# Eleven passes with barriers made into one continuous program, with an order of its own for each engine

## The reference, cut to what matters

```
x: [16, 256, 128]
for attn, ffn in ((geo, moe0), (diff, feed-forward + mx), (lora, moe2), (wide, moe3)):
    x = x + attn(norm(x))
    x = x + ffn(norm(x))
geo:  8 heads of 16, causal, a head-wise bias folded into q and k
diff: differential attention across the 32 half heads inside one token, then RMS norm; feed-forward 512; mx-quantised linear
lora: 16 heads of 8, not causal
wide: 16 heads with keys of 128, causal
moe0 / moe2 / moe3: top-1 routing to 8 / 14 / 8 experts, hidden 512 / 256 / 128 (Relu, Gelu, Relu)
moe3: an expert keeps only its first 512 tokens over all sequences, in order
```

## Time and profile before

| | us |
|---|---|
| device time, 3 runs: median | 2933.23 |
| lowest, highest | 2922.30, 2940.96 |
| span of the profiled execution, first to last instruction | 2937.0 |
| TensorE busy | 1974.8 (67%) |
| VectorE busy | 1762.4 (60%) |
| ScalarE busy | 1132.8 (39%) |
| GpSimd busy | 705.2 (24%) |

### The profile page before, as it was taken

How to read it: one execution, slowest core, us unless ns; L and a number is a source line. 1 busy time by engine, 2 the same in 40 slices (tenths; PEclk the granted TensorE clock), 3 DMA queues, 4 the chain that set the end, 5 groups by cost and what they waited for, 6 DMA issues and landing times. The chain is left out here.

```text
span 2937.0 us, 40367 instructions
## 1 busy us (share of the span) xinstructions
PE 1974.8 (67%) x12945; PEld 1381.7 (47%) x12945; DVE 1762.4 (60%) x4295; ACT 1132.8 (39%) x2730; POOL 705.2 (24%) x891
## 2 busy tenths in 40 slices
PE   4555655666978677766776678658775766657593
PEld 4233353345546544564456445645464335435452
DVE  2112856685768576857687667757685777543232
ACT  0112222332555336542554256425542353234261
POOL 1000431143014411442035203530243034100101
PEclk9757566568988788887898788879787876778695
DMA  9112031034103510352026201530153103301502
GB/s 249 24 46 74 1 110 32 1 98 136 23 29 106 150 35 2 107 158 53 2 73 183 62 2 47 173 84 16 39 153 100 22 1 100 89 9 33 142 1 60
DMA packets 183309, 207.84 MB, mean 71 GB/s; under 512 B 19792, under 2 KB 148432, under 8 KB 182640
## 3 DMA queue, kind: packets, MB, share of 16 engines
q1 hardware_dynamic: 165536, 186.19, 23.1%
q0 software_dynamic: 6144, 12.60, 1.4%
q10 hardware_dynamic: 11392, 6.18, 1.0%
HBM read 158.39 MB, written 42.34 MB: 68 GB/s over the span
## 5 line engine op out<-in xcount | busy, mean ns | idle before, releaser
L1450 POOL TENSOR_TENSOR second_room<-second_room 128x512 f32<-128x512 f32 x32 | 47.6, 1486 | 765.1 <-ACT second_room L1332 765.0
L1220 ACT ACTIVATE late_room<-ps,late_neg_max 128x128 f32<-128x128 f32 (+1 forms) x512 | 186.9, 420 | 69.2 <-DVE late_neg_max L1597 63.8
L1622 DVE TENSOR_REDUCE mid_room<-ps 128x2 f32<-128x512 f32 x256 | 165.1, 687 | 55.2 <-PE ps L954 52.0
L1257 ACT ACTIVATE mid_room<-ps 128x512 f32<-128x512 f32 x256 | 142.9, 598 | 132.0 <-PE ps L965 131.8
L1211 ACT ACTIVATE late_room<-ps 128x384 f32<-128x384 f32 x256 | 125.9, 492 | 155.1 <-PE ps L885 151.9
L1596 DVE TENSOR_REDUCE late_neg_max<-ps 128x1 f32<-128x128 f32 x256 | 73.5, 287 | 179.7 <-PE ps L877 179.1
L1779 DVE TENSOR_TENSOR second_room<-second_room 128x1024 f32<-128x1024 f32 x128 | 163.0, 1274 | 13.2 <-ACT second_room L1332 9.7
L1057 PE MATMUL ps<-mid_pool 128*128 128x128 f32 x544 | 107.2, 328 | 87.1 <-DMA mid_pool<-moe_tables 78.0
L875 PE MATMUL ps<-late_aT,heads_T 128*128 128x256 f32 x512 | 164.1, 405 | 0.0
L1783 DVE TENSOR_REDUCE second_room<-second_room 128x256 f32<-128x1024 f32 x128 | 156.2, 1220 | 4.4
L965 PE MATMUL ps<-mid_pool 51*128 51x256 bf16 x512 | 64.7, 338 | 130.9 <-DMA mid_pool<-max_rows 62.2
(11 more groups left out here) (389 smaller groups left out, 5174.4 us busy)
## 6 DMA issues: line engine op xcount, KB each, us to landing
early_pool<-moe_tables SPq DMA_DIRECT2D x88, 578.0 KB
mid_pool<-moe_tables SPq DMA_DIRECT2D x136, 321.0 KB
heads_T<-moe_tables SPq DMA_DIRECT2D x88, 192.5 KB
mid_pool<-mid_room SPq DMA_DIRECT2D x192, 64.0 KB
mid_room<-moe_sorted_in SPq DMA_DIRECT2D x32, 256.0 KB, 3.1
moe_sorted_out<-mid_room SPq DMA_DIRECT2D x32, 256.0 KB
early_room<-moe_sorted_in SPq DMA_DIRECT2D x16, 256.0 KB, 3.1
moe_sorted_out<-early_room SPq DMA_DIRECT2D x16, 256.0 KB, 5.8
```

The costliest lines, as they stand in the source:

```text
L1220: ins = act.activation(probs[s][:, n % RING, qt, 0:w], ps[:, bank, qt * P:qt * P + w], ACT.Exp, bias=neg_max[s][:, n % RING, qt:qt + 1])
L1257: act.activation(probs_T[s][:, n % (2 * QUAD), :], ps[:, B + slots.index(("unit", n)) % s.score_banks(at), :], ACT.Exp)\
L1622: dve.tensor_reduce(all_max[:, :, (h % 2 * 8 + h // 2) * GROUP_SEQS + seq], ps[:, B + n % s.banks, :].rearrange("p (q k) -> p q k", q=2), ...
```

## The change

The passes, the loop, the barriers, the copies of x and the clearing of semaphores are gone. Semaphores now count through the whole program: each is declared with the number of signals it gets per group, and `nth` gives the value to wait for in group g. x lives in a ring of five groups (`xs`, `x_of`), in which all four streams add in place; the next group's x is loaded at the start of EARLY's steps of the group before, and the result is sent from the ring.

Preparation is a fifth stream "P" whose steps stand among EARLY's. x of group 0 and the five loads that EARLY needs come first, then those of moe0, of SECOND, and at last those of MID and LATE. The copies of the tables of moe2 and moe3 stay on ScalarE's queue: its order begins "EEEPP", and they are the second P. On VectorE the order begins "PEPEEPEEPPEPP", on TensorE "EEEEPEEEP", with the 16 products of `wide_m` behind 50 more steps.

`ORDERS` now has one string per engine for the whole program (TensorE 2467 steps, ScalarE 1906, VectorE 1800, GpSimd 217, SP 468). There are no empty steps, and steps are finer (scores, transposes and products with values are steps of their own). Each stream works on group after group without any meeting point. Within the strings the stream with the older group mostly comes first.

Smaller edits: the octets of `back_to_tokens` go one by one instead of in waves; `gate_of_max` of moe0 and moe2 stands behind the signal `slots_ready`; small tiles are shared (`filled`, `starts`, `ends`, `table_of`, `dsq` inside `dhalves`, `max_rows` inside `mid_room`); `result` and the semaphore `result_free` are gone.

```diff
-        def next_turn():
-            nc.gpsimd.dma_reset(range(group_first.num, group_last.num + 1))
-            nc.all_engine_barrier()
-            nc.sync.sem_clear(range(group_first.num, group_last.num + 1))
-            nc.all_engine_barrier()
...
-        with nc.Fori(0, GROUPS - 3) as g:
-            with nc.Block(no_gpsimd_drain=True) as block:
-                group_block(block, list(STREAMS), x_v[:, bass.ds(g * TILES + 3 * TILES, TILES), :],
-                            out_v[:, bass.ds(g * TILES, TILES), :])
-            next_turn()
...
-                for source, target in ((MID, LATE), (SECOND, MID), (EARLY, SECOND)):
-                    if source in streams:
-                        settle()
-                        link(dve.tensor_copy(x[target][:, :, :], x[source][:, :, :]))
...
+def take_steps(engine, programs):
+    running = {letter: itertools.chain.from_iterable(rounds) for letter, rounds in programs.items()}
+    for letter in ORDERS[engine]:
+        next(running[letter])
...
+        def nth(told, g, n):
+            return told, g * a_round[told.name] + n
...
+        xs = sb("xs", [P, X_RING, TILES, DIM])
+        x_of = lambda g: xs[:, g % X_RING, :, :]
...
+        def steps_of(prepare, early, second, mid, late):
+            rounds = {"P": [prepare()]}
+            for s, program in ((EARLY, early), (SECOND, second), (MID, mid), (LATE, late)):
+                rounds[s.letter] = [program(g) for g in range(GROUPS)]
+            return rounds
...
+                def load_x(g):
+                    if g >= 1:
+                        sp.wait_ge(*nth(x_here, g - 1, 16))
+                    if g >= X_RING:
+                        sp.wait_ge(*nth(x_sent, g - X_RING, 16))
+                    sp.dma_start(x_of(g), x_v[:, g * TILES:(g + 1) * TILES, :]).then_inc(x_here, 16)
...
+                def prepare():
+                    act.wait_ge(prepared, LAM_SUMMED)
+                    act.activation(lam_exp[:, :], lam_sum[:, :], ACT.Exp).then_inc(lam_exped, 1)
+                    yield
+                    act.wait_ge(m0_here, 16 * len(m0_loads))
+                    act.wait_ge(second_here, 16 * len(second_loads))
+                    for dst, src in m2_copies + m3_copies:
+                        with nc.allow_non_contiguous_dma(reason="columns of tables, once"):
+                            act.dma_start(dst, src).then_inc(later_built, 16)
+                    yield
...
+                        if n < at.units:
+                            scores(n)
+                            yield
                         if TURN_LAG <= n < at.units + TURN_LAG:
                             turn_probs(n - TURN_LAG)
-                        last = n - VALUES_LAG
-                        if last >= 0 and last % QUAD == QUAD - 1:
-                            values(last // QUAD)
-                        yield
+                            yield
+                        quad, rest_of_quad = divmod(n - VALUES_LAG, QUAD)
+                        if rest_of_quad == QUAD - 1 and quad >= 0:
+                            values(quad)
+                            yield
```

More of the change, by code:

```diff
@@ L21 @@
 GROUPS = SEQS // GROUP_SEQS
+X_RING = 5
 BANK = 512
@@ L109, in score_banks @@
         return self.banks if at is LORA else self.banks - 1
[L111 to L119, removed]
+EARLY = Stream("geo", "E", 0, 2, ["geo_in", "geo_out", "moe0_router"], ["v", "o"])
+SECOND = Stream("diff", "S", 2, 1, ["diff_in", "diff_out", "diff_ff", "mx_in"], ["conn", "ff", "mx"])
+MID = Stream("lora", "M", 3, 2, ["lora_in", "lora_out", "moe2_in"], ["v", "o"])
+LATE = Stream("wide", "L", 5, 3, ["wide_in", "wide_out", "moe3_router"], ["v", "o"])
 STREAMS = (EARLY, SECOND, MID, LATE)
@@ L206, in sequence_model @@
+def take_steps(engine, programs):
+    running = {letter: itertools.chain.from_iterable(rounds) for letter, rounds in programs.items()}
+    for letter in ORDERS[engine]:
+        next(running[letter])
+    for letter, program in running.items():
+        assert next(program, "over") == "over", f"{engine}: {letter} has more steps than the order"
 def sequence_model(nc, a, out):
@@ L700, in take_steps @@
-        def take_steps(streams, programs):
-            letters = "".join(s.name[0].upper() for s in streams)
-            order = ORDERS[letters] if len(streams) > 1 else letters * len(WEIGHTS[streams[0]])
-            for letter in order:
-                next(programs[letters.index(letter)])
-            for program in programs:
-                assert next(program, None) is None, "a program has more steps than weights"
-        def steps(n):
-            for _ in range(n):
-                yield
@@ L1362, in late @@
                                                 lambda b: wide_c[:, b:b + 1])
-                    yield from experts(s, MOE3, "moe3_router")
-                programs = {EARLY: early, SECOND: second, MID: mid, LATE: late}
-                take_steps(streams, [programs[s]() for s in streams])
+                    yield from experts(s, MOE3, g, "moe3_router")
+                take_steps("ACT", steps_of(prepare, early, second, mid, late))
             @block.gpsimd
@@ L1938, in sequence_model @@
[L1938 to L1943 removed]
+                    yield from experts(s, MOE3, g, "moe3_router", m3_br)
+                take_steps("DVE", steps_of(prepare, early, second, mid, late))
```

1443 lines of the change are left out of this document (699 added, 744 removed).

## The result

The changed kernel takes 3241.8 us (median of four runs, 3225.8 to 3245.1) against 2937.1 us before (2922.3 to 2944.1): 1.103 times as long, 95% interval 1.099 to 1.107. The forecast was 2603 us. The profiled execution has a span of 3243.4 us in a run of 3245.1.

The account below looks back on a forecast made before the run. No engine was taken to bound the whole span, but the row of passes, each as long as its slowest stream. 222 + 205 + 6 x 270 + 560 = 2607 us of span, so 2603 us; range 2450 to 2790.

Parts of the forecast that it names:

- item 3: Steady state, EARLY of groups 2 to 7: six periods T of 270 us each, at VectorE density 0.80.
- item 2: Second EARLY, beside SECOND and the beginning of MID: 187 us in the trace plus 18, so 205; bounds 187 and 240.
- item 1: Preparation and first EARLY: 38 us won, ending at 222 us, with ScalarE's table copies issued until about 62 us.
- The drain: SECOND, MID and LATE of group 7 at the end: 195, 215 and 150 us, sum 560, bounds 490 and 600.
- No pause at hand-overs: Where one group follows another: no stretch of 5 us without VectorE work at a seam.
- 61 table loads: ScalarE's function-table loads rise from 41 to 61, 1.283 us each; the extra cost 0 to 26 us, inside T's range.
- The wait for the maxima: TensorE before MID's second pass over its scores: 62.2 us in all, 7.8 a group; growth much beyond 8 would refute.
- (c): Rival, slower: written VectorE and TensorE orders leave engines standing when durations differ; T from 330, 2963 us; chance 0.08.
- (a): Rival: only the seams go, density between them being set by chains, not order; T = 293, 2741 us; chance 0.20.

Follow-up runs that it names:

- by progress: Changed kernel with lists rewritten by replay on measured durations; each engine takes the ready step of the stream least far in its own group: 2847.0 us.
- tuned: As by progress, with an offset and an exponent for each stream found by search over replays: 2732.4 us, 0.930 of before.
- the old order: Changed kernel's program with only the ORDERS strings differing, every engine following the order of the passes of the kernel before: 2894.9 us.
- two doses of age: The rule by progress with each stage ranked 0.2, or in the other kernel 0.4, of a group earlier per stage: 3071.0 and 3401.2 us.
- oldest first: Changed kernel with lists rewritten by replay on measured durations; each engine takes a ready step of the oldest group: 3395.6 us.
- three-quarters kernel: Changed program in the old order, with SECOND's steps moved into the first three quarters of every round: 3330.9 us.
- youngest first: Changed kernel with lists rewritten by replay on measured durations; each engine takes a ready step of the youngest group: 3393.2 us.

## Why the prediction was wrong

**The step that failed is the period (item 3).** I had counted from the orders that EARLY is served last, always runs, and that its latency is therefore the period. Then I sized the period by a density, the share of it in which VectorE is busy, 0.80, as if all lanes were full. A lane served last doesn't get a density; it gets what three others leave. Measured: 2158 us for the six periods where I had 1620, 538 of the 636 us by which the span missed 2607. The density was a result: at 356 us a period it is 0.61, by progress it is 0.73, tuned 0.76. That the cause is the rule in the lists is shown by the lists exchanged with the program kept: 306 us a period in the old order, 294 by progress, 340 and 383 with two doses of age. The sum's T of 270 was nearly in reach of this program (277), with another rule.

**Second EARLY (item 2).** 285.6 us against 205, upper bound 240. The same error: I took the earlier trace rows's EARLY beside SECOND, from a pass in which both took 187 us together, and added a tenth, though here SECOND goes first.

**The start (item 1).** The wait was named and sized too small. I had the issues end at 62 us; they ran from 34.3 to 83.1, 48.8 us in place of 41.7 in the earlier trace rows and 7 us later than before where I had them 7 us sooner, and the first EARLY ended at 243.6 and not at 222. The 38 us won were 16. That it was the queue is shown by moving the copies (46 us off the first EARLY).

**Right.** The drain: 171, 235 and 148 us, 554 together against 560. That the sum fits is partly luck: SECOND was 24 us shorter than its term and MID 20 us longer. No pause at hand-overs. 61 table loads, 1.283 us each in mean. The wait for the maxima did not grow: 14.3 us in all for the second pass over the scores (62.2 in the earlier trace rows). The waits that grew are others, those for `wide_z` and for EARLY's exponentials named above.

**The rivals.** (c) was the one that came true in sign, "oldest first puts LATE's and MID's steps ahead of those that are ready", at T = 360 and a chance of 0.08. But its mechanism, an engine standing because real durations differ from the written ones, was not the main cause: with measured durations the rule is slower still. To come out on the slow side of 2933 us at T = 360 is thus a hit of (c) by its number and not by its reason. The missing rival was the rule itself, for which the orders had the evidence: 11 of EARLY's 41 VectorE steps beside SECOND, though that count is a hint and no measure, as the three-quarters kernel shows. (a), that only the seams go, was also too good: in the old order the seam stayed thin without its barrier, T = 306 and not 293.

**Open.** How the lost time divides between VectorE crowded by SECOND and the other streams' lateness in the three-quarters kernel wasn't separated. Nor was how much of a longer period is the lower clock: it falls with the packing in all these kernels, and none changes one without the other. Why four kernels with replayed lists (oldest first, youngest first, by progress, tuned) came out 1 to 2% above my ranges is open too.

## What to carry to other kernels

Where lanes hold one item each, the period is the longest lane: in every kernel here at least one lane follows itself without a gap. So before forecasting from an engine's density, name the lane that is always busy and ask what its rank leaves it; a rule by age serves the latency of one item, and throughput wants all lanes at one pace. Merge streams by share of work done, so that a stream heavy on VectorE has one heavy on TensorE beside it; here that gave 294 us a period where the old order gave 306, and tuned paces 277. Removing a barrier gave a period nothing here until the order also let work cross it.

## What the runs showed of the hardware

A loss of overlap came with a lower clock and more TensorE time: the same instructions of four rounds took 1041 us at a mean granted clock of 0.72, 1003 at 0.74, and 909 at both 0.84 and 0.88. A load of ScalarE's function tables took 1.283 us each time, 61 times in the changed kernel. The eight table copies occupied the issuing queue for 0.7 to 16.8 us each, 48.8 us in all on ScalarE and from 46.8 to 82.1 us on SyncE.
